# One operand of every VectorE operation in three edge sweeps comes from PSUM

## What is computed

```python
# layer 0 (sweep A): one head
e = leaky_relu(a_src[src] + a_dst[dst], 0.2)
m = segment_max(e, dst); ex = exp(e - m[dst]); denom = segment_sum(ex, dst)
out = segment_sum((ex / denom[dst])[:, None] * h[src], dst)
# layer 1 (sweep B): the same with 4 heads of 32; each edge's logit also has a_edge = (edge_attr_13 @ W_edge) . att_edge
# layer 2: agg = segment_sum(edge_attr_128, dst), then three dense layers
# layer 3 (sweep rel): W_rel for each of 8 relations
msg = (x @ W_rel[r])[edge_type, src]
agg = segment_sum(msg, dst) / max(deg, 1);  out = relu(x @ W_self.T + b + agg)
```

## Time and the profile before

| | us |
|---|---|
| median of 3 runs | 8294.65 |
| lowest, highest | 8226.39, 8331.6 |
| profiled execution, its own time | 8378.33 |
| its span, first to last instruction | 8376.5 |
| busy: POOL, DVE | 5693.2 (68%), 3873.6 (46%) |
| busy: ACT, PE | 976.0 (12%), 583.0 (7%) |

### The profile page before, as it was taken

How to read it: one execution, slowest core, us unless ns; L and a number is a source line. 1 busy time by engine, 2 the same in 40 slices (tenths; PEclk the granted TensorE clock), 3 DMA queues, 4 the chain that set the end, 5 groups by cost and what they waited for, 6 DMA issues and landing times.

```text
span 8376.5 us, 30090 instructions
## 1 busy us (share of the span) xinstructions
PE 583.0 (7%) x2254; PEld 405.5 (5%) x2254; DVE 3873.6 (46%) x13120; ACT 976.0 (12%) x2890; POOL 5693.2 (68%) x5446
## 2 busy tenths in 40 slices
PE   1100000000000420000000000016700000000000
PEld 1100000000000320000000000013400000000000
DVE  6344554455545635555555555577422222222223
ACT  1121221122211120000000000055300000000000
POOL 4566666666765557777777777585277777777775
PEclk7555555555555655555555555558855555555555
DMA  4255555555655213333333333323432322322322
GB/s 161 81 170 186 179 194 171 187 185 181 209 170 182 60 58 98 99 99 98 99 99 100 99 94 99 97 61 110 188 97 88 95 94 92 97 92 92 97 92 87
DMA packets 293303, 1013.00 MB, mean 121 GB/s; under 512 B 103056, under 2 KB 120080, under 8 KB 230240
## 3 DMA queue, kind: packets, MB, share of 16 engines
q1 hardware_dynamic: 114192, 638.77, 20.1%
q0 software_dynamic: 175872, 369.49, 17.5%
q10 hardware_dynamic: 3024, 2.82, 0.1%
HBM read 511.47 MB, written 499.22 MB: 121 GB/s over the span
## 4 chain that ended last, share of the span: by engine, by line
DVE 28%; POOL 15%; issue 10%; another core or an unknown queue 6%; PE 3%; DMA 1%; POOLq 0%; ACT 0%; DVEq 0%; ACTq 0%; SPq 0%
DVE edge_rows L1770 19%; POOL edge_rows L849 12%; DVE edge_rows L995 3%; DVE old L989 2%; POOL node_sums L1050 2%; PE ps L1620 2%; POOL edge_rows L1719 1%; PE ps L1607 1%; DVE edge_rows L971 0%; DVE stats L1304 0%; PE ps L1661 0%; DVE edge_rows L942 0%; DMA edge_rows<-table_b,src_i 0%; DVE run_max L935 0%
## 5 line engine op out<-in xcount | busy, mean ns | idle before, releaser
L1719 POOL DMA_INDIRECT edge_rows<-table_rel,rel_row x1568 | 1650.2, 1052 | 645.3 <-issue 518.9
L849 POOL DMA_INDIRECT edge_rows<-table_b,src_i x1568 | 1662.5, 1060 | 618.0 <-issue 474.2
L849 POOL DMA_INDIRECT edge_rows<-table_a,src_i x1568 | 1563.8, 997 | 734.7 <-issue 470.2
L1770 DVE SCALAR_TENSOR_TENSOR edge_rows<-edge_rows,keep 128x128 f32<-128x128 f32 x1567 | 554.5, 354 | 1628.2 <-DVE edge_rows L1770 1097.1
L986 DVE SCALAR_TENSOR_TENSOR edge_rows<-edge_rows,weight_decay 128x129 f32<-128x129 f32 x1567 | 546.9, 349 | 307.8 <-DVE attrs L1011 179.5
L1011 DVE SCALAR_TENSOR_TENSOR attrs<-attrs,keep 128x128 f32<-128x128 f32 x1567 | 544.0, 347 | 303.7 <-DVE edge_rows L986 168.6
L995 DVE TENSOR_TENSOR edge_rows<-edge_rows,old 128x132 f32<-128x132 f32 x1567 | 460.4, 294 | 381.6 <-remote 149.1
L989 DVE TENSOR_TENSOR old<-edge_rows,weight_decay 128x132 f32<-128x132 f32 x1567 | 459.1, 293 | 351.8 <-remote 179.7
L894 ACT ACTIVATE weight_decay<-weight_decay 128x32 f32<-128x32 f32 (+1 forms) x196 | 52.8, 269 | 4027.5 <-remote 1435.1
L902 ACT ACTIVATE edge_rows<-edge_rows,weight_decay 128x129 f32<-128x129 f32 x1568 | 470.1, 389 | 3.2
L917 DVE TENSOR_TENSOR z<-edge_rows,dst_logit 128x16 f32<-128x16 f32 (+1 forms) x196 | 39.2, 200 | 472.8 <-DMA edge_rows<-table_b,src_i 258.6
(11 more groups left out here) (293 smaller groups left out, 3000.9 us busy)
## 6 DMA issues: line engine op xcount, KB each, us to landing
sums_b<-edge_rows SPq DMA_DIRECT2D x98, 1120.0 KB
sums_a<-edge_rows SPq DMA_DIRECT2D x98, 1040.0 KB
attrs<-in_ea SPq DMA_DIRECT2D x98, 1024.0 KB
sums_attr<-attrs SPq DMA_DIRECT2D x98, 1024.0 KB
sums_rel<-edge_rows SPq DMA_DIRECT2D x98, 1024.0 KB
table_rel<-rel SPq DMA_DIRECT2D x98, 512.0 KB
edge_rows<-table_a,src_i POOLq DMA_INDIRECT x1568
edge_rows<-table_b,src_i POOLq DMA_INDIRECT x1568
```

Of the source, the lines that this page charges most:

```text
L849: e.indirect_dma_start(out=rows[:, s, c, :], out_offset=None, in_=L.table, in_offset=bass.IndirectOffsetOnAxis(ap=src[:, g * GC + c:g * GC ...
L1719: e.indirect_dma_start(out=rows[:, s, c, :], out_offset=None, in_=table_rel, in_offset=bass.IndirectOffsetOnAxis(ap=rel_row[:, g * GC + c: ...
L1770: i = e.scalar_tensor_tensor(rows[:, s, c, :], before, keep[:, g * GC + c:g * GC + c + 1], rows[:, s, c, :], ALU.mult, ALU.add)
```

## The change

The group's 16 columns are cut into `NQ` = 4 quarters of `QC` = 4. The eight banks of PSUM, which these stages hardly use, take one operand of each DVE operation:

- A: ACT writes the weighted rows into banks 0 to 3 (a bank for each quarter) instead of back to SBUF, and signals once per quarter; it copies each quarter of `attrs` into bank 4 or 5, and the gathered logits into bank 6. There are two Exp a group, one to SBUF and one to PSUM. The running sum of the weights, until now column 128 of the rows, is a scan of its own.
- B: ACT copies the gathered logits and the edge logits into bank 6 and puts the exponents into bank 0 or 1. DVE writes the product (`old`) into bank 5.
- A and B: the leaky ReLU is two operations, with the scaled value in bank 7; the running maximum is copied to bank 7 for the difference; `edge_proj` lies in bank 7.
- rel: ACT copies each gathered quarter into bank 0 to 3, and DVE takes the rows from there.
- DVE's order: `logits(g + 1)` now stands behind all sums of group g, in place of taking turns with them. A DVE bank is written again only when its quarter of the group before has been summed.
- `summed` and `attr_summed` count quarters, so the waits of POOL and SP on them are scaled by 4. Some semaphores of other stages share a name.

The diff, cut to its core:

```diff
     def attention_edges(L, sb, dst_l, edge_logit, attr=None, feat_dram=None, proj=None):
...
+        def column_bank(c):
+            return ps[:, c // QC, (c % QC) * D:(c % QC + 1) * D]
+        def attr_bank(q):
+            return ps[:, 4 + q % 2, 0:QC * D]
+        def exp_bank(g):
+            return ps[:, g % 2, 0:2 * GC * H].rearrange("p (c h) -> p c h", h=H)
+        def old_bank(c):
+            return ps[:, 5, (c % 2) * 160:(c % 2) * 160 + NW].rearrange("p (h k) -> p h k", h=H)
...
         def scalar(e):
+            def logits_of_rows(g):
+                s = g % NS
+                if L.AE:
+                    e.activation(edge_bank, edge_logit[:, cols(g), :], ACT.Copy)
+                e.wait_ge(*gathered[s].at(16 * GC * (g // NS + 1)))
+                e.activation(logit_bank, rows[:, s, :, L.M0:L.M0 + H], ACT.Copy).then_inc(logits_in.sem, 1)
...
+            def weights(g):
+                e.wait_ge(*exped.at(g + 1))
+                for q in range(NQ):
+                    if g:
+                        e.wait_ge(*summed.at((g - 1) * NQ + q + 1))
+                    for c in range(q * QC, (q + 1) * QC):
+                        i = e.activation(column_bank(c), rows[:, g % NS, c, 0:D], ACT.Copy,
+                                         scale=wd[:, g % 2, c:c + 1])
+                    i.then_inc(weighted.sem, 1)
...
+                    e.activation(attr_bank(q), attrs[:, g % NA, q * QC:(q + 1) * QC, :].rearrange("p c d -> p (c d)"),
+                                 ACT.Copy).then_inc(attr_in.sem, 1)
...
         def vector(e):
...
-                t = then(e.scalar_tensor_tensor(z[:, b, :, :], z[:, b, :, :], SLOPE, z[:, b, :, :], ALU.mult,
-                                                ALU.max))
+                t = then(e.tensor_scalar(slope_bank, z[:, :, :], SLOPE, None, ALU.mult))
+                e.wait_ge(*step.at(t))
+                t = then(e.tensor_tensor(z_bank, z[:, :, :], slope_bank, ALU.max))
...
+                t = then(e.tensor_copy(run_bank, run[:, b, 0:GC, :]))
+                then(e.tensor_tensor(wd_in[:, b, 0:GC, :], z_bank, run[:, b, 1:GC + 1, :], ALU.subtract))
+                e.wait_ge(*step.at(t))
+                t = then(e.tensor_tensor(run_bank, run_bank, run[:, b, 1:GC + 1, :], ALU.subtract))
...
+                then(e.tensor_tensor_scan(R[:, :, D], wd[:, b, GC:2 * GC], ones_bank(g), init, ALU.mult, ALU.add))
...
+                        i = e.scalar_tensor_tensor(R[:, c, 0:D], before, wd[:, b, GC + c:GC + c + 1], column_bank(c),
+                                                   ALU.mult, ALU.add)
...
+                    t = then(e.tensor_tensor(old_bank(c), before.rearrange("p (h k) -> p h k", h=H),
+                                             bc(exp_bank(g)[:, GC + c, :].unsqueeze(2), [P, H, C + 1]), ALU.mult))
+                    e.wait_ge(*step.at(t))
+                    i = e.tensor_tensor(num[:, c, :, :], num[:, c, :, :], old_bank(c), ALU.add)
...
-            for g in range(NG):
-                both = [running_sums(g)] + ([logits(g + 1)] if g + 1 < NG else [])
-                while both:
-                    both = [i for i in both if next(i, "over") != "over"]
+            for g in range(NG):
+                if H == 1:
+                    sums_of_one_head(g)
+                else:
+                    sums_of_heads(g)
+                if g + 1 < NG:
+                    logits(g + 1)
...
     def edges_rel_stage(local, own_part):
...
+            for g in range(NG):
+                e.wait_ge(*gathered[g % NS].at(16 * GC * (g // NS + 1)))
+                for q in range(NQ):
+                    if g:
+                        e.wait_ge(*summed.at((g - 1) * NQ + q + 1))
+                    e.activation(ps[:, q, 0:QC * D],
+                                 rows[:, g % NS, q * QC:(q + 1) * QC, :].rearrange("p c d -> p (c d)"), ACT.Copy
+                                 ).then_inc(copied.sem, 1)
...
-                    i = e.scalar_tensor_tensor(rows[:, s, c, :], before, keep[:, g * GC + c:g * GC + c + 1],
-                                               rows[:, s, c, :], ALU.mult, ALU.add)
+                        i = e.scalar_tensor_tensor(rows[:, s, c, :], before, keep[:, g * GC + c:g * GC + c + 1], data,
+                                                   ALU.mult, ALU.add)
```

More of the change, by code:

```diff
@@ L18 @@
 GC = 16
+QC = 4
 BIG = 1.0e30
@@ L242, in __init__ @@
             self.filled = sem_of("table_filled", NK)
-            self.stored = [sem_of(f"table_stored{i}", 16 * turns(NK, 2, i)) for i in range(2)]
+            self.stored = [sem_of(f"rows_stored{i}", 16 * turns(NK, 2, i)) for i in range(2)]
             self.logits_stored = sem_of("table_logits_stored", 16)
@@ L846, in gpsimd @@
                 if g >= NS - 1:
-                    e.wait_ge(*summed.at(g - NS + 2))
+                    e.wait_ge(*summed.at((g - NS + 2) * NQ))
                 for c in range(GC):
@@ L898, in scalar @@
                 if H == 1:
-                    R = rows[:, g % NS, :, :]
-                    e.wait_ge(*exped.at(g + 1))
-                    for c in range(GC):
-                        e.activation(R[:, c, 0:NW], R[:, c, 0:NW], ACT.Copy,
-                                     scale=wd[:, g % 2, c, :]).then_inc(weighted.sem, 1)
+                    weights(g)
                 if g + 1 < NG:
+                    logits_of_rows(g + 1)
                     exponents(g + 1)
@@ L975, in running_sums, with sums_of_heads @@
+            def sums_of_heads(g):
+                s = g % NS
+                R = rows[:, s, :, :]
+                num = R[:, :, 0:NW].rearrange("p c (h k) -> p c h k", h=H)
+                e.wait_ge(*exped.at(g + 1))
+                then(e.tensor_tensor(num, num, bc(exp_bank(g)[:, 0:GC, :].unsqueeze(3), [P, GC, H, C + 1]),
+                                     ALU.mult))
                 for c in range(GC):
@@ L997, in running_sums @@
-                    if c < GC - 1:
-                        t = then(i)
+                        e.wait_ge(*summed.at(g * NQ))
+                    before = rows[:, s, c - 1, 0:NW] if c else rows[:, (g - 1) % NS, GC - 1, 0:NW]
+                    e.wait_ge(*step.at(step.n))
+                    if c and c % QC == 0:
+                        e.wait_ge(*summed.at(g * NQ + c // QC))
+                    t = then(e.tensor_tensor(old_bank(c), before.rearrange("p (h k) -> p h k", h=H),
+                                             bc(exp_bank(g)[:, GC + c, :].unsqueeze(2), [P, H, C + 1]), ALU.mult))
@@ L1019, in vector @@
-            for _ in logits(0):
-                pass
-            for g in range(NG):
-                both = [running_sums(g)] + ([logits(g + 1)] if g + 1 < NG else [])
-                while both:
-                    both = [i for i in both if next(i, "over") != "over"]
-            e.wait_ge(*summed.at(NG))
+            logits(0)
+            for g in range(NG):
+                if H == 1:
+                    sums_of_one_head(g)
+                else:
+                    sums_of_heads(g)
+                if g + 1 < NG:
+                    logits(g + 1)
@@ L1350, in nodes_b_stage @@
         rel = sb("rel", [P, NSR, NREL, D])
-        rel_stored = [sem(f"rel_stored{i}") for i in range(NSR)]
+        rel_stored = [sem_of(f"rows_stored{i}", 16 * turns(NJ, NSR, i)) for i in range(NSR)]
         nodes = AttentionNodes(B, sb, node_b, lambda k: out_b[:, k % 3, :, :])
@@ L1776, in vector @@
                         i.then_inc(summed.sem, 1)
-            e.wait_ge(*summed.at(NG))
+            e.wait_ge(*summed.at(NG * NQ))
             crossing.vector(e)
@@ L1785, in nodes_rel_stage @@
         out_ready = sem("out_ready")
-        out_stored = [sem(f"out_stored{i}") for i in range(3)]
+        out_stored = [sem_of(f"rows_stored{i}", 16 * turns(NK, 3, i)) for i in range(3)]
         def gpsimd(e):
```

193 lines of the change are left out of this document (101 added, 92 removed).

## The result

The changed kernel took 8523.22 us (median of 4 runs, 8511.45 to 8537.31) against 8299.47 us for the kernel before (4 runs): a ratio of 1.0283, 95% interval 1.0213 to 1.0353. It is slower; 7450 us and a range up to 8400 had been forecast. The profiled execution spans 8522.4 us, 146 us more than the profiled one before; that one was slower than its own median, so the two profiles show 146 us of a loss of 224.

A forecast was written before the change was run, and what follows sets the result against it. POOL, with 1568 gathers a sweep, was taken as the bound; 335 + 310 + 214 us over its floor plus 40 at sweep ends, 899 in all, off 8378.3 gave 7479, stated as 7450 us; range 7370 to 8400.

The forecast's parts named there:

- (1): Sweeps A, B and rel: no DVE operation keeps two SBUF inputs, so gathers are no longer stretched; 440 us gained.
- (2): All three sweeps: DVE's slow 1.40 us rhythm, taken as port sharing with POOL, goes with the operand; 420 us, bounds 0 to 420.
- (3): DVE's group length with serial logits: B 17.8, A 13.4, rel 7.5 us, all under POOL's 19.96, so cost 0.
- R3: Rival: sweep B becomes DVE-bound by its PSUM writes, 7630 us; chance 0.13.
- (4): ACT's added copies in A and rel stay hidden, 7.9 us a group in A, 2.4 of 20 in rel; cost 0.
- (5): Waits and queues: POOL and SP keep their DMA order, waits count quarters, renamed semaphores cost nothing.
- (6): Ends of sweeps B and rel: with no backlog after the last gather, 20 us off each, bounds 0 and 35.
- (R2): Rival: DVE's logits in B and A; late increments stay, the serial chain makes them dear; 8800, by 1% less 8710; chance 0.20.

The follow-up runs named there:

- the spaced runs: Six runs with POOL memsets between gathers to slow them to 1.40 us: 7392.45, 7413.79, 8470.53 us (small memsets), 8193.34, 8332.81, 8437.9 us (one long memset per eight gathers).
- only the long operations relieved: Kernel before, with only B's exponents and edge_proj moved to PSUM, so two long DVE products have one SBUF input: 8559.14 us, 1.0262; again 8576.82 us, 1.0281.
- before, with fewer increments: Kernel before; in A one increment per column for two operations, in B four one-head operations with one increment per column: 8563.17 us, 1.0263.
- before, with pauses: Kernel before, operands in SBUF, plus a 128x1500 memset on POOL behind every eighth gather in A and B: 8437.9 us, 1.0099.
- interleaved, with pauses: Changed kernel with logits taking turns with the sums, plus a 128x1500 POOL memset behind every eighth gather in A and B: 8193.34 us, 0.9798 to the kernel before.
- logits behind the sums, with pauses: Changed kernel, its order kept, plus a 128x1500 POOL memset behind every eighth gather in A and B: 8332.81 us, 0.9971 to the kernel before.

## Why the prediction was wrong

What most of the runs support is a pile behind POOL, in late sessions. Something there takes one gather per 1.40 us. POOL issues one per 1.2475 us when nothing holds it. What it is ahead grows; while a few gathers are piled up, DVE starts its operations only every 0.70 or 1.40 us, and goes on so until the pile has gone, POOL idle or not. The kernel before can be read again with it. In A, POOL issued its first 80 gathers in 99.9 us; at 1.40 us each 71 would have gone, so 9 are left, 12 us of work. The timeline of the kernel before, after that 80th gather:

```profile
478.09 0.94 POOL L849 DMA_INDIRECT edge_rows<-table_a,src_i  x1 [0.30 <-issue]
...
488.69 0.35 DVE L1011 SCALAR_TENSOR_TENSOR attrs<-attrs,keep 128x128 f32<-128x128 f32 x1 [0.98 <-DVE edge_rows L986]
489.46 0.35 DVE L986 SCALAR_TENSOR_TENSOR edge_rows<-edge_rows,weight_decay 128x129 f32<-128x129 f32 x1 [0.42 <-DVE attrs L1011]
489.73 0.35 DVE L1011 SCALAR_TENSOR_TENSOR attrs<-attrs,keep 128x128 f32<-128x128 f32 x1
```

POOL's gather ends at 479.03, DVE is late until 489.5, 10.5 us on. In rel POOL is never made to wait, so the pile grows to its limit and the gathers themselves are held to 1.40 us; the earlier trace rows has DVE still late after the last one. What takes the 1.40 us no row shows. It isn't the transfers, for while DVE is late behind the 80th gather the DMA engines stand still (the last two numbers are DMA share and GB/s):

```profile
480.00:489.00 9.00, 0.00 (x0) 0.00 (x0) 2.57 (x7) 0.00 (x0) 0.00 (x0) 0.50 0.00 0
```

The pile is inferred from such times and from the spaced runs. The traces allow one more test. Count 1.40 us for each gather from its start, one after the other, and call late a DVE operation with 0.33 to 2.6 us of idle time before it that neither ACT nor a DMA ended. In B of the changed kernel 583 of the 630 operations that start with 4 us or more of the pile left are late, and 101 of the 2364 that start with under 2 us. In B of the kernel before it is 354 of 560, and 21 of 3193. The late operations between the first and the last gather, beside POOL's waits for a sum:

| | late in A, B | waits in A, B (us) |
|---|---|---|
| before | 609, 519 | 248, 129 |
| changed | 1125, 998 | 335, 439 |
| changed, logits interleaved | 632, 883 | 340, 341 |
| only the long operations relieved | 706, 837 | 340, 432 |
| before, with fewer increments | 535, 341 | 299, 311 |
| before, with pauses | 0, 0 | 0, 0 |
| interleaved, with pauses | 0, 0 | 0, 0 |
| logits behind the sums, with pauses | 1203, 725 | 60, 40 |
| changed, prompt session | 0, 4 | 0, 0 |

The counts compare only roughly from one order of operations to another: with fewer increments there are fewer late operations and more waits. And two things don't fit a pile with one fixed threshold. In the run with the pauses and the logits behind the sums, 1131 of A's 1203 late operations start with under 2 us of the pile left. In rel of the kernel before only 2 of the first 69 operations are late, while the pile grows to 12 us. So the pile says when lateness comes in most of the runs, but not all of what it needs.

Now my steps in turn.

(1) *The stretching goes.* Right for A and B: 0.944 us in the mean. The Trainium skill ("SBUF — State Buffer", section "Who interferes with whom") states that a DVE instruction with at most one SBUF input, outside the 2-port modes, doesn't contend with GpSimd. A and B agree, with 0.944 us in late and prompt sessions alike. For rel it was the wrong attribution: of its 171 us over 1479 nothing went (1655 us), since these gathers are held by the pile and not by L1770; in the prompt session they take 1479 us. And I treated the stretching as pure loss. In B of the kernel before it spaced the gathers to (1662 + 474) / 1568 = 1.36 us and so kept the pile small for over 100 us at a time. Taking it away fed the pile, and of the 269 us that (1) counted for A and B nothing was kept: the waits grew by 87 and 310 us.

(2) *The slow rhythm goes.* This is the step that failed. I took the late steps for POOL and DVE taking turns at a shared port, to go with the second SBUF input. With no such input left they stayed in rel (2168.5 us against 2169.2) and nearly doubled in A and B (1125 and 998 against 609 and 519), and POOL's waits rose to 335 and 439 us in place of falling to nothing. It carried 420 us of the sum, and it decided about the 269 us of (1) too, since a shorter gather is worth something only if POOL doesn't wait the longer for it. I called it the weak step, named the two rows that spoke against it (L1758's increment, 2.57 us late with a PSUM operand, by the code, for the row itself names no releaser; DVE still slow after POOL's last gather), said that they looked like a queue, and took the other end all the same. The second row alone spoke against a lock between two busy engines, for one of them was idle.

(3) *DVE's length per group.* Sound: in the prompt session no group of A or B keeps POOL waiting, and a DVE write to PSUM takes 0.300 us where I had no row (L1070 in the late session, 128x132) against 0.293 into SBUF. Rival R3 is out.

(4), (5) *ACT and the queues.* As said; ACT's 702 us in A and 234 us in rel ended no wait of POOL.

(6) *The ends.* 10 us longer behind A and B and 1.5 behind rel, where I had taken 20 off each of B and rel: DVE is still in late steps there.

(R2) *The rival on the slower side* had the place (DVE's chain in B while late steps last), and was given 0.20. Its price was too high, 8710 us against 8523: it had 71 us for a slow group of B, and the trace has two groups in 49. And it priced the serial logits alone; put back, they gave about 90 us in B and left a loss of 1.2%. That rest it didn't have: a faster POOL brings more late steps, as the run with only two long operations relieved shows in the old order (1.026, and 837 late operations in B against 519).

The sum of 7479 us was one for a prompt session: where nothing comes late, the kernel takes 7381 us, 3.8% less than the one before, which takes 7670. That the two sums lie so close is in part luck, since the other stages are shorter there too (the first sweep begins at 327 us in place of 374), which no step of mine had.

## What to carry to other kernels

Before counting an engine's waits as gain, ask what sets its long-run rate: here no sweep's 1568 gathers took less than 2168 us in a late session, while the sum assumed 1956, and rel's even 22.4 us a group was the row that showed it. A delay that outlasts the work of the engine blamed for it points to a queue and not to a conflict, and a queue is best fed no faster than it drains: here two edits that each lost (1.012 and 1.010) gained 2% together, though with the other order of the logits the same spacing gained almost nothing (0.997). And an edit near such a balance can change its sign from one session to the next, 0.962 and 1.028 here, so two kernels have to be compared in more than one.

## What was not expected of the hardware

- The same kernel takes 8299 to 8362 us in some sessions and 7669 us in others; the profiles differ by DVE's late steps and rel's 1.40 us a gather, against 1.2475 for the changed kernel, and by shorter stages elsewhere too (the changed kernel's first sweep begins at 374 us in a late session, at 327 in a prompt one).
- In late sessions, DVE's operations that wait for nothing also start on a grid of 0.70 us while gathers are piled up.
- Shortening the gathers' own time by 47 and 164 us, with nothing else of weight changed, raised the waits by 93 and 304 us.
- Memsets of one byte behind a gather are free up to the 0.30 us of idle time there (1957 us a sweep with one and without), and 9 of them take 0.35 us together and bring a gather every 1.44 us.
